# Low parts of the activations made on GpSimd instead of VectorE, with GpSimd's gathers written out between them

## What is computed

```python
e = jnp.stack([tbl_0[ids[:, 0]], tbl_1[ids[:, 1]], tbl_2[ids[:, 2]], tbl_3[ids[:, 3]], tbl_4[ids[:, 4]]], axis=1)
...
def _ple_layer(x, W, b, Gw, Gb, Gsw=None, Gsb=None):
    xe = x[:, EXPERT_IN_IDX, :]
    eo = jax.nn.relu(jnp.einsum('bed,edh->beh', xe, W) + b)
    gates = jax.nn.softmax(jnp.einsum('btd,tdk->btk', x[:, :T, :], Gw) + Gb, axis=-1)
    sel_eo = eo[:, SEL, :]
    task_out = jnp.einsum('btk,btkh->bth', gates, sel_eo)
    if Gsw is None:
        return task_out
    gs = jax.nn.softmax(x[:, T, :] @ Gsw + Gsb, axis=-1)
    shared_out = jnp.einsum('be,beh->bh', gs, eo)
    return jnp.concatenate([task_out, shared_out[:, None, :]], axis=1)
...
h = _ple_layer(inputs, W0, b0, G0w, G0b, Gs0w, Gs0b)
z = _ple_layer(h, W1, b1, G1w, G1b)
h = jnp.concatenate([z, dense_ctx], axis=1)
h = jnp.maximum(h @ W_top1 + b_top1, 0.0)
h = jnp.maximum(h @ W_top2 + b_top2, 0.0)
y = h @ W_top3
```

## Time and profile before

| | |
|---|---|
| median of 3 timed runs | 2047.74 us (2043.83 to 2049.45) |
| the profiled execution's own time | 2042.9 us |
| its span, first to last instruction | 2041.1 us |
| TensorE busy | 2013.5 us, 99% |
| VectorE busy | 1372.1 us, 67% |
| ScalarE busy | 716.4 us, 35% |
| GpSimd busy | 169.2 us, 8% |
| granted TensorE clock, mean | 0.999 |

### The profile page before, as it was taken

How to read it: one execution, slowest core, us unless ns; L and a number is a source line. 1 busy time by engine, 2 the same in 40 slices (tenths; PEclk the granted TensorE clock), 3 DMA queues, 4 the chain that set the end, 5 groups by cost and what they waited for, 6 DMA issues and landing times.

```text
span 2041.1 us, 26192 instructions
## 1 busy us (share of the span) xinstructions
PE 2013.5 (99%) x8832; PEld 1640.8 (80%) x8832; DVE 1372.1 (67%) x1427; ACT 716.4 (35%) x964; POOL 169.2 (8%) x152
## 2 busy tenths in 40 slices
PE   7999999999999999999999999999999999999999
PEld 6878787888878888888887787888888888888887
DVE  4579888887256765658555888887953667566564
ACT  3333233323333333333434333323233332423343
POOL 4631000000030002111033000000000000000000
PEclk9999999999999999999999999999999999999999
DMA  6544333333343334334344333243333323332321
GB/s 194 171 147 124 114 93 116 90 126 101 97 138 110 107 94 136 118 125 123 93 145 133 115 93 122 84 134 110 101 102 93 107 90 119 98 112 94 113 94 42
DMA packets 70003, 230.44 MB, mean 113 GB/s; under 512 B 12398, under 2 KB 12654, under 8 KB 69948
## 3 DMA queue, kind: packets, MB, share of 16 engines
q1 hardware_dynamic: 61688, 208.75, 32.6%
q0 software_dynamic: 7488, 20.98, 3.2%
q10 hardware_dynamic: 772, 0.09, 0.0%
HBM read 229.56 MB, written 0.23 MB: 113 GB/s over the span
## 4 chain that ended last, share of the span: by engine, by line
PE 88%; DVE 5%; issue 3%; DMA 3%; ACT 1%; SPq 0%; ACTq 0%; POOL 0%; DVEq 0%
PE main L336 26%; PE main L338 26%; PE main L337 26%; PE top L336 3%; PE top L337 3%; PE top L338 3%; DVE w_lo L769 1%; DMA gate_b<-gates_dram 1%; PE gps L373 1%; PE gps L371 1%; DVE prod L844 1%; DMA gates_dram<-logit_t 1%; DVE eo_b L844 1%; ACT w_hi L478 0%; DMA eo_sh<-in_tbl,idx 0%
## 5 line engine op out<-in xcount | busy, mean ns | idle before, releaser
L336 PE MATMUL main<-act_hi,w_hi 128*128 128x512 f32 x2568 | 1002.1, 390 | 15.5 <-DVE w_lo L769 9.4
L337 PE MATMUL main<-act_lo,w_hi 128*128 128x512 f32 x2568 | 1000.1, 389 | 0.0
L338 PE MATMUL main<-act_hi,w_lo 128*128 128x512 f32 x2568 | 1000.1, 389 | 0.0
L769 DVE TENSOR_TENSOR w_lo<-raw,w_hi 128x1024 fp32r<-128x1024 f32 (+1 forms) x356 | 433.7, 1218 | 555.1 <-ACT w_hi L478 554.9
L478 ACT ACTIVATE w_hi<-raw 128x1024 fp32r<-128x1024 f32 (+1 forms) x356 | 376.3, 1057 | 1117.4 <-PE main L338 1016.4
L336 PEld LDWEIGHTS main<-act_hi,w_hi 128*128 128x128 f32 x2568 | 482.2, 188 | 132.3 <-issue 11.1
L338 PEld LDWEIGHTS main<-act_hi,w_lo 128*128 128x128 f32 x2568 | 482.4, 188 | 101.3
L337 PEld LDWEIGHTS main<-act_lo,w_hi 128*128 128x128 f32 x2568 | 482.3, 188 | 99.6
L850 DVE TENSOR_TENSOR slots<-slots,prod 128x1024 f32<-128x1024 f32 (+1 forms) x200 | 244.8, 1224 | 5.9
L327 POOL DMA_INDIRECT slots<-in_tbl,idx x144 | 165.1, 1147 | 929.9 <-DVE act_lo L781 616.9
L844 DVE TENSOR_TENSOR prod<-eo_sh,gate_b 128x1024 f32<-128x1024 f32 x136 | 165.7, 1218 | 4.7 <-DMA gate_b<-gates_dram 2.8
(11 more groups left out here) (67 smaller groups left out, 584.2 us busy)
## 6 DMA issues: line engine op xcount, KB each, us to landing
raw<-in_w SPq DMA_DIRECT2D x320, 512.0 KB, 3.6
gate_b<-gates_dram SPq DMA_DIRECT2D x34, 512.0 KB, 4.7
raw<-in_w_top SPq DMA_DIRECT2D x32, 512.0 KB, 3.5
gate_b<-gates_dram SPq DMA_DIRECT2D x16, 256.0 KB, 4.3
slots<-in_tbl,idx POOLq DMA_INDIRECT x144, 3.5
raw<-in_w_top SPq DMA_DIRECT2D x4, 256.0 KB, 2.7
eo_b<-in_dense SPq DMA_DIRECT2D x2, 192.0 KB, 2.7
gates_dram<-logit_t SPq DMA_DIRECT2D x18, 12.0 KB
```

What stands on the lines that cost most here:

```text
L336: nc.tensor.matmul(dst, lhs_hi, rhs_hi, start=start, stop=False)
L337: nc.tensor.matmul(dst, lhs_hi, rhs_lo, start=False, stop=False)
L338: return nc.tensor.matmul(dst, lhs_lo, rhs_hi, start=False, stop=stop)
L769: nc.vector.tensor_tensor(w_lo[0:parts, slot, 0:cols], raw[0:parts, rawslot, 0:cols], w_hi[0:parts, slot, 0:cols], ALU.subtract).then_inc( ...
```

## The change

VectorE's `hand_over` is taken out, and all 216 subtractions of the hand-overs stand in GpSimd's queue as `low`, with the same operands and the same waits for `act_hi_rdy`. GpSimd's loop over gathers is written out: `gather` issues what one turn of the loop issued, and the calls of `low` stand between. The gather of table 3 for the first half comes behind the first hand-over, and those of the second half behind the hand-overs named in the code. The first activations of all, and the small ones of the tower (`first_outputs`), stay on VectorE. TensorE's, ScalarE's and SyncE's code is untouched.

```diff
+            def low(S, chunk, x=False):
+
+                for k in range(KT):
+                    pool.wait_ge(act_hi_rdy, S * KT + k + 1)
+                    if x:
+                        lo, src, hi = as_subs(act_lo[:, k, :]), x_strip(chunk, k), as_subs(act_hi[:, k, :])
+                    else:
+                        lo, src, hi = act_lo[:, k, :], slots[:, chunk + k, :], act_hi[:, k, :]
+                    nc.gpsimd.tensor_tensor(lo, src, hi, ALU.subtract).then_inc(act_lo_rdy, 1)
+
             for h in range(HALVES):
-                for t in X_ORDER[h]:
...
+                s0 = steps(h)[1]
+                for t in ((2, 3) if h else (0, 1, 2)):
+                    gather(h, t)
+                low(s0 + 1, 0, x=True)
+                if h == 0:
+                    gather(0, 3)
+                for t in range(1, T):
+                    low(s0 + 1 + t, t * KT, x=True)
+                low(s0 + T + 1, T * KT)
+                low(s0 + T + 2, 0)
+                if h == 0:
+                    gather(1, T)
+                for n in range(T - 1):
+                    low(s0 + T + 3 + 2 * n, (n + 1) * KT)
+                    if h == 0 and n:
+                        gather(1, n - 1)
+                    low(s0 + T + 4 + 2 * n, n * KT)
+                low(s0 + T + 3 + 2 * (T - 1), (T - 1) * KT)
+                if h == 0:
+                    low(steps(1)[0], T * KT, x=True)
...
-            def hand_over(S, chunk, ks, x=False):
-
-                for k in ks:
-                    dve.wait_ge(act_hi_rdy, S * KT + k + 1)
...
-                    nc.vector.tensor_tensor(lo, src, hi, ALU.subtract).then_inc(act_lo_rdy, 1)
...
                 split_lo(U, 0, off, V)
                 b2, b3 = ops[1](2), ops[1](3)
                 if shared:
-                    hand_over(S, chunk, range(0, 6))
                     run(b3[:2])
-                    hand_over(S, chunk, (6, 7))
                     split_lo(U + 1, 1, off + 1, V)
                     return b2[2:] + b3[2:]
-                hand_over(S, chunk, range(KT), x=x)
                 split_lo(U + 1, 1, off + 1, V)
                 run(b2 + b3)
```

More of the change, by code:

```diff
@@ L313, in _, with gather @@
                       2: [later + u for u in (1, 3, 5, 7)], 3: [later + u for u in (9, 10, 12, 13)]})
-            for h in range(HALVES):
-                for t in X_ORDER[h]:
[L316 to L329, removed]
+            def gather(h, t):
+                turn = x_turn(h, t)
+                if h:
+                    pool.wait_ge(act_lo_rdy, read[t] * KT)
+                for bt in range(NBT):
+                    if turn:
+                        pool.wait_ge(x_in[bt], 16 * Q4 * turn)
+                    if begin[h][t][bt]:
+                        pool.wait_ge(unit_done, begin[h][t][bt])
+                    for s in range(Q4):
+                        c = NBT + ((t * HALVES + (h if t < T else 0)) * NBT + bt) * Q4 + s
+                        at = (bt * Q4 + s) * (D // Q4)
+                        pool.indirect_dma_start(
+                            x_rows(t)[:, at:at + D // Q4], None, tables[t].rearrange("v (q n) -> (v q) n", q=Q4),
+                            bass.IndirectOffsetOnAxis(ap=idx[:, c:c + 1], axis=0)).then_inc(x_in[bt], 16)
@@ L956, in step, with change @@
                         run(now[cut:] if second else now[:cut])
-            def change(U, V, off, S, chunk, ops, shared=False, x=False):
+            def change(U, V, off, ops, shared=False):
                 split_lo(U, 0, off, V)
@@ L965, in change, with tower_slots @@
                 if shared:
-                    hand_over(S, chunk, range(0, 6))
                     run(b3[:2])
-                    hand_over(S, chunk, (6, 7))
                     split_lo(U + 1, 1, off + 1, V)
                     return b2[2:] + b3[2:]
-                hand_over(S, chunk, range(KT), x=x)
                 split_lo(U + 1, 1, off + 1, V)
                 run(b2 + b3)
-            def tower_slots(U, V, off, S, chunk, last=False, x=False):
+            def tower_slots(U, V, off):
                 for j in (1, 2):
@@ L978, in tower_slots @@
                 split_lo(U + 4, 0, off, V + 1)
-                if not last:
-                    hand_over(S, chunk, range(KT), x=x)
-                    split_lo(U + 5, 1, (off + 1) % RAW, V + 1 + (off + 1) // RAW)
+                split_lo(U + 5, 1, (off + 1) % RAW, V + 1 + (off + 1) // RAW)
             def first_outputs(S, ks=range(MT1)):
@@ L1042, in _ @@
                 if h == 0:
-                    change(U, U // RAW, U % RAW, s0 + 1, 0, ops, x=True)
+                    change(U, U // RAW, U % RAW, ops)
                 else:
@@ L1048, in _ @@
                     run(ops[1](2))
-                    change(U + 2, (U + 2) // RAW, off, s0 + 1, 0, (None, lambda p: ops[1](3) if p == 3 else []), x=True)
+                    change(U + 2, (U + 2) // RAW, off, (None, lambda p: ops[1](3) if p == 3 else []))
                 def task0(t, plan, last=False, x={}):
@@ L1055, in task0 @@
                     step(U, V, off, ops, (q0 + 1 + t, NG, t * 2), (q0 + 2 + t, NG), plan, x=x)
-                    return change(U + STEP, V + STEP // RAW, off, s0 + 2 + t, (t + 1) * KT, ops, shared=last, x=not last)
+                    return change(U + STEP, V + STEP // RAW, off, ops, shared=last)
                 for t in range(T - 1):
@@ L1064, in _ @@
                 U = u0 + U_T1
-                V, S = U // RAW, s0 + T + 2
-                change(U, V, off, S, 0, (None, lambda p: []))
+                V = U // RAW
+                change(U, V, off, (None, lambda p: []))
                 E, Pb, Q = e0 + (T + 2) * STEP, p0 + 8 * (T + 1), q0 + T + 1
@@ L1070, in _ @@
                 step(U, V, off, ops, (Q, NG), (Q + 1, NG))
-                change(U + STEP, V + STEP // RAW, off, S + 1, KT, ops)
+                change(U + STEP, V + STEP // RAW, off, ops)
                 Un, Vn, both = U + STEP, V + STEP // RAW, STEP + MT1
                 def task1(n, split, last=False):
-                    t, Sn, Ut, Vt = n + 1, S + 1 + n * 2, Un + n * both, Vn + n * (both // RAW)
+                    t, Ut, Vt = n + 1, Un + n * both, Vn + n * (both // RAW)
                     ops = gating("layer1", t, E + STEP + n * STEP, Q + 1 + n, h, Pb + 8 + n * 8)
                     step(Ut, Vt, off, ops, (Q + 1 + n, NG), split, x=turns[h].get("L", {}) if last else {})
-                    change(Ut + STEP, Vt + STEP // RAW, off, Sn + 1, (t - 1) * KT, ops)
-                    tower_slots(Ut + STEP, Vt + STEP // RAW, off, Sn + 2, (t if last else t + 1) * KT)
+                    change(Ut + STEP, Vt + STEP // RAW, off, ops)
+                    tower_slots(Ut + STEP, Vt + STEP // RAW, off)
                 with dve.Fori(0, T - 2) as n:
@@ L1089, in _ @@
                 if more:
-                    tower_slots(U, U // RAW, off, steps(h + 1)[0], 4 * KT, x=True)
+                    tower_slots(U, U // RAW, off)
             for m in range(MT1 - 2):
```

5 lines of the change are left out of this document (removed).

## The result

The changed kernel takes 2142.92 us (median of 4 runs, 2140.61 to 2145.45) against 2048.45 us before (2043.83 to 2049.45): ratio 1.0475, 95% interval 1.0462 to 1.0487. It is slower by 94 us. The forecast was slower, 2134 us, range 2060 to 2190.

A forecast was written before the change was run, and what follows sets the result against it. TensorE's own matmul stream was taken as the kernel's length, late operands adding to it. Hand-over losses of 86.5 us on the profiled 2042.9 gave 2129.4, carried over to the timed median as 2134 us; range 2060 to 2190.

The forecast's parts named there:

- likeliest case: GpSimd's subtractions and VectorE's two-SBUF-input operations alternate behind hand-overs: 86.5 us lost, 2093 to 2188 us, chance 0.50.
- Does the change help VectorE?: Behind hand-overs, VectorE without the subtractions (4.90 us each) still waits for the same w_hi; relief costed at nothing.
- Gathers and ISA row: In GpSimd's queue, the gathers' new places cost nothing; the new ISA row comes once, at the first subtraction.
- g: Length of one subtraction on GpSimd: taken as 1.2 us, likely 1.0 to 1.4.
- The two alternate: Behind hand-overs, GpSimd and VectorE take turns when both want to run, 1.2 us for each operation.
- Layer 0 pays what VectorE is held: At six hand-overs inside layer 0, VectorE is held 4.3 us without slack and TensorE pays it: 25.8 us.
- Just-in-time hand-overs: Seven hand-overs (four tower to gated step, two from the shared step, one into the second half): 0 us.
- no exclusion: Rival: both engines run freely, gated steps hide the subtractions, towers still pay; 17 us, 2065 us, chance 0.18.
- GpSimd keeps the port: Rival: at hand-overs GpSimd's eight follow each other and VectorE waits for all; 51 us, 2099 us, chance 0.15.
- VectorE keeps it: Rival: the last three subtractions wait for VectorE's row to run out; about 157 us, 2205 us, chance 0.08.

The follow-up runs named there:

- half: The changed kernel with each GpSimd subtraction covering only the first 256 of 512 columns: 2046.54 us, ratio 1.0012 to the kernel before.
- hold: The changed kernel with VectorE waiting for all eight low parts of a hand-over before its second w_lo: 2123.26 us, ratio 1.0383.
- psum_after: The changed kernel, VectorE's 128x1024 operations reading one operand from PSUM: 2067.14 us; control, the kernel before with the same replacement: 2044.85 us.
- filler: The changed kernel with 20 more matmuls, result unread, in the first unit of each of six towers: 2133.30 us, ratio 1.0430.
- after_again: The changed kernel unaltered, run again on the chip of filler as its measure: 2141.79 us, ratio 1.0471.

## Why the prediction was right

Its likeliest case came: direction, mechanism and size (2134 forecast, 2142.92 measured). By its own steps:

- **"Does the change help VectorE?" Costed at nothing.** Right. The second `w_lo` keeps its distance of 6.5 us, and half shows a VectorE rid of the work at no gain. One sign came out otherwise: VectorE's busy time fell by 63 us, not by its 216 low parts (132.5), because its other operations ran longer.
- **Gathers and ISA row costed at nothing.** Right: half has both, and its ratio is 1.0012. Between the last gather and the first subtraction GpSimd idles 0.72 us.
- **g = 1.2 us.** In hold the subtractions follow each other 1.25 us apart (eight in 10.07 us), just over the value taken.
- **The two alternate.** Right, by psum_after and hold. The rows of the kernel before could show one half of it, that GpSimd waits for VectorE; that VectorE waits for GpSimd too was an assumption there. What VectorE takes of it was sized too long: a pair of operations takes 2.2 us, not 2.4. With g a little too short, the two errors work against each other: the eight end after 12.90 us at a tower, 13.2 by my numbers.
- **Layer 0 pays what VectorE is held.** Right: VectorE's fourth gating operation starts 8.71 us behind the second `w_lo` and in half 4.89, so it was held 3.8 us (I had 4.3), and the six hand-overs cost 3.4 to 4.4 each. TensorE's waits for `w_lo` grew from 9.4 to 17.4 us. With those for GpSimd's low parts they are 64.5 us, where I had some 80.
- **Just-in-time hand-overs cost 0.** 1.5 us for seven.
- **What was missing: the clock.** By the estimates above 17 to 20 us of the 102 are the lower level's; only the share of the six towers was tried (8.5 us by filler). Without this term the measured sum is 82 to 85, against 86.5 forecast; so the 16 us by which the total lies above my sum are this term. That the whole came so near is in part luck: the pair sized too long hides some of what was missing.

The rivals: "no exclusion" was costed at 17 us, and psum_after, where VectorE has one SBUF input, loses 22 to its control. "GpSimd keeps the port" was costed at 51 us; hold forces that order and loses 79, with the lower clock and the held `w_lo` in the towers on top. In the changed kernel neither happens: there subtractions 6 to 8 and VectorE's operations take turns. "VectorE keeps it" is excluded by the same rows.

## What to carry to other kernels

Before work is moved off an engine, look at what ends the wait behind it: here ScalarE's `w_hi` did, so there was nothing to win. TensorE needed each chunk every 0.68 or 1.14 us and the new engine made one in 1.25. A subtraction on GpSimd was not free of VectorE: beside operations of VectorE with two SBUF inputs it came every 2.2 us for 1.25, and they took 2.2 to 2.3 us for 1.22. The slower order reached an operand (`w_lo`) that the change never touched. When TensorE waits for an engine that isn't full, that engine's order may be the cause: five changed lines of a plan gave 0.76%, where moving 216 instructions lost 4.75%.

## What the runs showed of the hardware that was not expected

- Behind each of the six towers TensorE's clock fell to its lower level, for 3.4 or 6.8 us (up to 10.2 in after_again), after TensorE had worked in bursts of three matmuls with waits of 0.3 to 1.3 us between them. 20 matmuls more in each of these towers kept it up, and these 120 made the kernel 8.5 us faster. In psum_after the waits between the bursts were 0.3 us, and the clock did not fall there.
- GpSimd's indirect DMAs too wait for a VectorE operation with two SBUF inputs: their mean falls from 1147 to 980 ns when one input lies in PSUM. VectorE's operations don't get longer by it (a mean of 1218 ns for `w_lo` in both kernels).
- In the alternation an operation of VectorE adds 0.95 us to GpSimd's pace (1.25 to 2.2) though it takes 1.22 us alone. So the exclusion does not last for all of the time that the profile gives for it.
